# In the odd slots of the attention stage, PE turns the probabilities ahead of the value tile instead of behind it

## What is computed

```
h = tokens(x)                                  # 32 clips x 93 rows x 256: two layers and a batch norm
h = h + attn(layernorm(h))                     # 16 heads of 64
h = h + ffn(layernorm(h))                      # a shared expert and 8 routed ones, the best 2 for each row

def attn(x):
    q, k, v = (einsum('bsm,hmd->bhsd', x, kernel[i]) for i in range(3))
    p = softmax(einsum('bhsd,bhtd->bhst', q, k) * scale, axis=-1)
    out = einsum('bhst,bhtd->bhsd', p, v)
    return transpose_and_merge_heads(out) @ WO[0]
```

## Time and profile before

| | |
|---|---|
| Time, median of 3 runs | 1101.61 us (1101.18 to 1101.79) |
| Time of the profiled execution | 1100.58 us |
| Its span | 1098.9 us |
| Mean granted clock of PE | 0.978 |
| PE busy | 1030.9 us (94%), 8364 instructions |
| PEld busy | 955.9 us (87%) |
| DVE busy | 621.4 us (57%) |
| ACT busy | 511.2 us (47%) |
| POOL busy | 421.2 us (38%) |

### The profile page before, as it was taken

How to read it: one execution, slowest core, us unless ns; L and a number is a source line. 1 busy time by engine, 2 the same in 40 slices (tenths; PEclk the granted TensorE clock), 3 DMA queues, 4 the chain that set the end, 5 groups by cost and what they waited for, 6 DMA issues and landing times. The chain is left out here.

```text
span 1098.9 us, 24220 instructions
## 1 busy us (share of the span) xinstructions
PE 1030.9 (94%) x8364; PEld 955.9 (87%) x8365; DVE 621.4 (57%) x1619; ACT 511.2 (47%) x1130; POOL 421.2 (38%) x535
## 2 busy tenths in 40 slices
PE   5994999999999999999999799999999999997998
PEld 5993798888888887888888699999999999997998
DVE  3664666767777675867757755433334444353464
ACT  3542554444544545444444455444445555444252
POOL 2000231335252443525343250606660646264882
PEclk9996999999999999999999699999999999998999
DMA  9516999800010000001011153332344323312553
GB/s 186 129 41 208 358 345 345 277 16 17 29 28 28 23 33 14 14 28 28 28 22 40 47 163 99 108 130 64 121 134 134 111 79 129 110 58 70 154 149 104
DMA packets 104628, 115.32 MB, mean 105 GB/s; under 512 B 29856, under 2 KB 94848, under 8 KB 104576
## 3 DMA queue, kind: packets, MB, share of 16 engines
q1 hardware_dynamic: 75936, 73.82, 22.2%
q0 software_dynamic: 18176, 29.12, 9.3%
q10 hardware_dynamic: 10464, 11.70, 3.3%
HBM read 51.53 MB, written 62.95 MB: 104 GB/s over the span
## 5 line engine op out<-in xcount | busy, mean ns | idle before, releaser
L1232 POOL TENSOR_TENSOR prob<-prob,rc 93x372 f32<-93x372 f32 x128 | 103.0, 805 | 315.5 <-DVE rc L1127 315.1
L1787 DVE TENSOR_TENSOR act_s<-up_ps,act_s 128x384 fp32r<-128x384 f32 (+1 forms) x168 | 81.7, 493 | 176.5 <-ACT up_ps L1634 175.2
L866 PE MATMUL pj_ps<-xg,wA 128*128 128x372 f32 x768 | 153.3, 346 | 7.8 <-DVE xg L704 5.0
L866 PEld LDWEIGHTS pj_ps<-xg,wA 128*128 128x128 f32 x768 | 129.7, 191 | 18.0 <-DVE xg L704 4.9
L1632 ACT ACTIVATE act_s<-up_ps 128x384 fp32r<-128x384 f32 (+1 forms) x168 | 73.8, 439 | 148.6 <-PE up_ps L1525 144.2
L854 PE MATMUL pj_ps<-wB,xg 128*93 128x512 f32 x384 | 102.7, 403 | 0.0
L1023 ACT ACTIVATE probT<-t_ps 93x372 f32<-93x372 f32 x128 | 60.7, 474 | 90.1 <-PE t_ps L887 89.6
L1131 DVE TENSOR_TENSOR oT<-o_ps,oT 128x372 fp32r<-128x372 f32 x64 | 34.8, 544 | 106.1 <-ACT oT L1028 105.7
L1525 PE MATMUL up_ps<-rx,wB 128*128 128x256 f32 (+1 forms) x576 | 86.4, 309 | 0.7 <-issue 0.7
L1539 PE MATMUL dn_ps<-wB,act_s 128*128 128x256 f32 x720 | 85.7, 279 | 0.0
L1525 PEld LDWEIGHTS up_ps<-rx,wB 128*128 128x128 f32 x576 | 83.6, 188 | 1.6 <-issue 0.9
(11 more groups left out here) (196 smaller groups left out, 1965.5 us busy)
## 6 DMA issues: line engine op xcount, KB each, us to landing
slots<-zeros SPq DMA_DIRECT2D x8, 3072.0 KB, 23.0
y_rows<-zeros SPq DMA_DIRECT2D x5, 2688.0 KB, 20.8
rows_in<-slots SPq DMA_DIRECT2D x22, 384.0 KB, 3.5
y_rows<-rows_out ACTq DMA_DIRECT2D x22, 384.0 KB, 2.6
raw<-in_L_ffn_routed_up POOLq DMA_DIRECT2D x7, 1024.0 KB, 5.4
raw<-in_L_ffn_routed_down POOLq DMA_DIRECT2D x7, 1024.0 KB, 8.2
ln_out<-split SPq DMA_DIRECT2D x8, 744.0 KB, 3.3
frames<-in_x SPq DMA_DIRECT2D x8, 400.0 KB
```

The lines of the kernel that those rows point to most:

```text
L866: ins = pe.matmul(pj_ps[:, t, 0:N], wA[:, wp, at:at + P], xg[:, dp, m, :], start=(k == 0), stop=(k == 5))
L1232: pool.tensor_tensor(p, p, rc[:, u % 2, :].unsqueeze(2).broadcast_to([TP, 4, SL]), ALU.mult).then_inc(scaled, 1)
L1787: dve.tensor_tensor(act_s[:, LO, f, 0:width], up_ps[:, f % 4, 0:width], act_s[:, HI, f, 0:width], ALU.subtract).then_inc(ract_lo, 1)
```

## The change

In the six odd slots that have a value tile (1, 3, 5, 7, 9, 11) PE issues `turn` first and the value tile behind it. ACT's list is changed in the same way; ACT copies a value tile in two odd slots only (v10 in slot 5, v12 in slot 9), and there `take_turned` comes ahead of `take_v`. The even slots, DVE's list and POOL's list are as they were. No instruction is added, removed or resized.

```diff
@@ PE, group(g, behind, ahead) @@
                         if s == 14 and ahead:
                             pe.wait_ge(taken[1], number(g, "z11"))
                             qk_tile(g, "q0")
-                        if s in V:
+                        if s % 2 == 0 and s in V:
                             v_tile(g, V[s])
                         if s == NU - 1 and behind:
                             rank_tile(pe, g, g - 1)
@@
                             turn(g, s - 2)
                         elif behind:
                             turn(g - 1, NU + s - 2)
+                        if s % 2 and s in V:
+                            v_tile(g, V[s])
                         if s == NU - 1 and ahead:
                             qk_tile(g, "k0")
@@ ACT, group(g, behind, ahead) @@
-                        if s in V:
+                        if s % 2 == 0 and s in V:
                             take_v(g, "v" + V[s])
                         if s >= 2:
                             take_turned(g, s - 2)
                         elif behind:
                             take_turned(g - 1, NU + s - 2)
+                        if s % 2 and s in V:
+                            take_v(g, "v" + V[s])
```

## The result

| | before | after |
|---|---|---|
| Median of 5 runs | 1101.61 us (1099.99 to 1102.03) | 1111.71 us (1110.70 to 1115.24) |
| Profiled execution: time, span | 1100.58, 1098.9 us | 1111.37, 1109.8 us |
| PE busy in the span | 1030.9 us (94%) | 1033.1 us (93%) |

The account below looks back on a forecast made before the run. PE bounds a middle group, busy 62.70 of 65 us, so its added waits go into the end time. Terms 2.8 + 4.2 + 1.5 + 1.5 + 0.3 + 1.9 = 12.2 us gave a median of 1113.8 us, range 1106.5 to 1118.

Parts of the forecast that it names:

- rival B: Slots 12 to 15: delay paid back where PE waits anyway, only groups 0 and 7 pay, about 2 to 3 us, 1104; chance 0.10.
- Step 1: Slot 9, groups 1 to 7: z20 waits longer for ACT's copy of v12, same bank, no turn covering it; 2.8 us.
- Step 2: Slots 5 and 7, groups 1 to 7: the turn waits for POOL; the two delays don't add, the greater counts; 4.2 us.
- bounds of 2.4 to 6.4 us: Slots 5 and 7: cost if all seven groups were short (2.4 us) or all seven long (6.4 us).
- the short form: Slots 5 and 7: a group pays 0.35 us, the small DVE instruction not held by POOL's indirect DMA.
- the long form: Slots 5 and 7: a group pays 0.92 us, the small DVE instruction taking 0.71 us and ending with POOL's indirect DMA.
- it was let through: Groups 2 to 4, slots 5 and 7: claim that the small DVE instruction was not held up by POOL's indirect DMA.
- Steps 3 and 4: Group 0, slot 5: turn waits for POOL's unit 3, +1.5 us; group 7, slot 3: v03 follows the waiting turn, +1.5 us.
- Step 5: Slot 6: q of pair 4 behind v10, same bank, a hairline wait of 0 to 0.1 us, 8 times; 0.3 us.
- Step 6: 47 odd slots: a turn right behind values is slower, 0.04 us each, 1.9 us, with ends -1 and +3.8.
- Rival D: Group 7, slot 3: the clock falls after a 2.2 us standstill, 5.8 us at half speed costs 2.9 us, 1116.7; chance 0.08.

## Why the prediction was right, point by point

**What bounds the stage.** Right. Every wait added to PE came out in the time, and no mark shows any of it paid back (rival B). The tie of DVE's list to PE was the row that decided this.

**Step 1, slot 9.** The mechanism was right, the size 0.42 us instead of the 0.33 measured. Behind a turn the value tile starts after 0.35 us and not 0.42, so its end moved less than I had it. z20's wait is 0.68 us in group 3, where I had 0.77.

**Step 2, slots 5 and 7.** Right in both sizes, 3.9 us against 4.2, and in that the two don't add. The rule of the Trainium skill ("SBUF — State Buffer", "SBUF: two separate sides") that DVE and GpSimd hold their shared port pair as an exclusive lock agrees with the run in which POOL's DMAs were moved (0.71 against 0.16 us for the same DVE instruction). The bounds of 2.4 to 6.4 us were worth having: group 3 paid the short form in one kernel and the long form in the next.

That "it was let through" in groups 2 to 4 is only half of it: there the next instruction, line 48, was long. A shift of a tenth, which I made the condition, isn't needed: group 3 changed from the short form to the long one with the DMA 0.58 us ahead of line 679 in both traces.

**Steps 3 and 4.** Right: 1.4 and 1.8 us against 1.5 and 1.5. In step 4 the scores came 1.76 us later and not 1.47 because the clock fell while the value tile ran: with the clock up the same slot gave 1.43 us.

**Step 5.** Nothing was lost there; it was hairline, as said.

**Step 6.** Wrong. The term of 1.9 us was taken from a row in which scores followed the turn. Behind a turn comes a value tile, and the pair takes 1.87 us against 1.89 in the old order: 0. I had named the lower end, and chose the middle between ends with nothing to say for it.

**Rival D.** It came true beside the forecast, at 1.5 us instead of 2.9 (1.13 behind slot 3 and 0.4 in it). The clock fell behind the wait of 2.16 us, but for 3.4 us and not for the 5.8 that I had from the stage's end. I also misread what led to it there: the granted clock is 1.00 from 612 to 614 us and 0.68 from 614 to 615, and the third wait that I named began at 615.2, so two waits had gone before the fall and not three. I had set D as a case of its own at 0.08, which was too low: the clock fell in three of the four traces that have this wait. The Trainium skill ("TensorE: Matmul & The Clock Gate", "What's actually happening") has TensorE's clock follow how busy it has been; that the same wait takes it down in one run and not in another fits its remark, made there of the clock's rise, that the point of change varies from run to run.

**The sum.** 12.2 us forecast, 10.56 by the marks. Too high by 1.9 (step 6), 0.5 (step 1), 0.3 each (steps 2 and 5) and 0.1 each (steps 3 and 4); too low by the 1.5 of the clock. The closeness of the total is in part luck, for step 6 and the clock nearly cancel. The group lengths tell the two apart: groups 2 to 4, where the clock stayed up, take 65.5 us from start to start and not the 65.8 or more that I had named.

## What to carry to other kernels

Where one engine is full, an instruction between two others is also their cover: before moving it, ask what copy or what other engine's result runs beneath it, and compare the release with the place where the work will be wanted, even where the trace shows no wait today. To take a wait away, put work of another bank between, and look one tile further, at who waits for that bank next. A sequence of common marks in two traces, with the difference of their differences, puts a change of one per cent into its slots where whole times scatter by as much as half of it.

## What was not expected of the hardware

A single idle piece of about 2.2 us on TensorE took the granted clock to its 1.2 GHz level for 3.4 us in three traces out of four, and cost 1.5 us; in the fourth, at 2.23 us, it stayed up. A DVE instruction of 0.16 us took 0.71 beside POOL's indirect DMA in some groups of a run, and in others the one behind it took 0.52 instead of 0.17, with the distance to the DMA between 0.57 and 0.59 us in all of them. What mattered for the time was not that one was held but whether the next one waits for its result.
